# One unit of the projection in another order: side 1 takes the values first and the output gate last, and ScalarE takes the output gate last

## The reference

```python
xn = _ln(x, norm_w, norm_b)
left = xn @ left_w + left_b
right = xn @ right_w + right_b
...
left = left * jax.nn.sigmoid(xn @ lgate_w + lgate_b)
right = right * jax.nn.sigmoid(xn @ rgate_w + rgate_b)
out_gate = jax.nn.sigmoid(xn @ ogate_w + ogate_b)
out = jnp.einsum('bkjd,bkid->bijd', left, right)
out = _ln(out, onorm_w, onorm_b)
out = out @ out_w + out_b
return out * out_gate
```

## Time and profile before

| what | value |
|---|---|
| median of 3 runs | 2826.93 us (2826.92 to 2828.26) |
| the profiled execution: its own time, its span | 2826.94 us, 2825.1 us |
| busy, share of the span | PE 86%, weight load 71%, VectorE 78%, ScalarE 49%, GpSimd 36% |
| the projection's units | from about 224 us to 1010 us of the span |

### The profile page before, as it was taken

How to read it: one execution, slowest core, us unless ns; L and a number is a source line. 1 busy time by engine, 2 the same in 40 slices (tenths; PEclk the granted TensorE clock), 3 DMA queues, 4 the chain that set the end, 5 groups by cost and what they waited for, 6 DMA issues and landing times. The chain is left out here.

```text
span 2825.1 us, 42511 instructions
## 1 busy us (share of the span) xinstructions
PE 2443.7 (86%) x14742; PEld 1994.7 (71%) x14742; DVE 2209.7 (78%) x3468; ACT 1380.1 (49%) x1812; POOL 1021.5 (36%) x1043
## 2 busy tenths in 40 slices
PE   0007999999999979999999996799999989979982
PEld 0006889998989868888888885566666666778872
DVE  6998999999999758888888888777676767438852
ACT  0106999999999956766766775122122222110000
POOL 0019888888898720000000000344444444300000
PEclk9999999999999989999999998899999999869997
DMA  9944999999999777777777777999999999539999
GB/s 383 388 186 178 348 354 350 348 349 344 351 345 348 284 291 272 281 288 273 282 287 277 279 284 299 335 404 416 394 417 393 415 391 393 131 116 407 421 420 410
DMA packets 244976, 927.49 MB, mean 328 GB/s; under 512 B 18009, under 2 KB 21593, under 8 KB 244442
## 3 DMA queue, kind: packets, MB, share of 16 engines
q1 hardware_dynamic: 205912, 796.12, 74.3%
q10 hardware_dynamic: 38898, 129.21, 11.4%
HBM read 527.85 MB, written 394.92 MB: 327 GB/s over the span
## 5 line engine op out<-in xcount | busy, mean ns | idle before, releaser
L1231 POOL TENSOR_TENSOR fi_square_sum<-fi_square_sum,fi_square 128x1024 f32<-128x1024 f32 x128 | 302.8, 2366 | 359.2 <-ACT fi_square L1197 359.2
L712 DVE SCALAR_TENSOR_TENSOR pj_lr<-pj_v_ps,keep_b_val,pj_sig 128x1024 f32<-128x1024 f32 x256 | 328.4, 1283 | 91.0 <-PE pj_v_ps L565 59.5
L1197 ACT ACTIVATE fi_square<-fi_x 128x1024 f32<-128x1024 f32 x128 | 135.5, 1059 | 515.8 <-DVE fi_x L1259 513.3
L505 POOL TENSOR_TENSOR front_ring<-front_ring,front_gn_shift 128x512 f32<-128x512 f32 x256 | 329.4, 1288 | 1.0 <-DVE front_ring L678 1.0
L1152 PE MATMUL fi_y_ps<-fi_scaled,keep_w_bd 128*128 128x512 f32 x512 | 273.0, 615 | 28.0 <-DVE fi_scaled L1242 27.2
L904 PE MATMUL ct_acc_ps<-ct_l_hi,ct_r_hi 128*128 128x512 f32 x1024 | 281.0, 395 | 17.1 <-ACT ct_r_hi L927 17.1
L648 ACT ACTIVATE pj_sig<-pj_g_ps,keep_b_gate 128x1024 f32<-128x1024 f32 x256 | 285.7, 1116 | 5.7 <-PE pj_g_ps L565 2.0
L908 PE MATMUL ct_acc_ps<-ct_l_lo,ct_r_hi 128*128 128x512 f32 x1024 | 280.7, 395 | 0.0
L912 PE MATMUL ct_acc_ps<-ct_l_hi,ct_r_lo 128*128 128x512 f32 x1024 | 280.1, 394 | 0.0
L1242 DVE TENSOR_TENSOR fi_scaled<-fi_m,fi_s_ps 128x512 f32<-128x512 f32 x256 | 173.7, 679 | 134.8 <-DMA fi_m<-mixed_d 124.7
L1223 POOL MEMSET fi_square_sum<- 128x1024 f32 x1 | 1.0, 951 | 747.0 <-POOLq L780 747.0
(11 more groups left out here) (183 smaller groups left out, 6288.6 us busy)
## 6 DMA issues: line engine op xcount, KB each, us to landing
lr_d<-pj_lr SPq DMA_DIRECT2D x128, 1024.0 KB, 6.1
gate_d<-pj_gout SPq DMA_DIRECT2D x128, 512.0 KB, 6.8
ct_l<-lr_d SPq DMA_DIRECT2D x64, 1024.0 KB, 7.0
ct_r<-lr_d SPq DMA_DIRECT2D x64, 1024.0 KB, 9.0
mixed_d<-ct_o SPq DMA_DIRECT2D x64, 1024.0 KB, 5.0
fi_g<-gate_d SPq DMA_DIRECT2D x128, 512.0 KB, 15.1
fi_x<-in_x SPq DMA_DIRECT2D x32, 2048.0 KB, 17.3
fi_m<-mixed_d SPq DMA_DIRECT2D x128, 512.0 KB, 17.6
```

The lines of the kernel that those rows point to most:

```text
L505: pool.tensor_tensor(tile(m), tile(m), keep.gn_shift[:, :].unsqueeze(1).to_broadcast([P, WS // 2, C]), ALU.add).then_inc(shifted, 1)
L712: dve.scalar_tensor_tensor(out=out[:, :, RG * (m % 2):RG * (m % 2) + RG], in0=v_ps[:, :].rearrange("p (q i) -> p q i", i=RG), scalar=keep. ...
L1231: pool.tensor_tensor(square_sum[:, :, :], square_sum[:, :, :], square[:, :, :], ALU.add).then_inc(sum_done, 1)
```

## The change

It edits the order of instructions in one unit of `project`. On TensorE, behind T0, side 1 takes its value products first and those of the output gate last. V1.0 now stands in front of S0, and carries the wait for `gated`; O1.0 keeps its wait for `half_o`, five products further on. On ScalarE the operations behind the sigmoid go from `copy_rest`, `gate`, `copy_turned` to `copy_turned`, `copy_rest`, `gate`. The semaphore `vals_in` now counts both sides, so the numbers in its waits double. No operation is added or removed.

```diff
             def values(n, m, e, i):
-                if e == 0 and i == 0:
+                if e == 1 and i == 0:
                     at_least(pe, gated, n)
                 last = one(v_ps[:, L * e:L * e + L], keep.w_val, m, e, i, i == 0, i == 2)
-                if e == 1 and i == 2:
+                if i == 2:
                     last.then_inc(vals_in, 1)
...
                 if here:
-                    out_gate(n, m, 1, 0)
+                    values(n, m, 1, 0)
                 if rest:
                     subtract_high(n + 2, m + 2, 0)
                 if here:
+                    values(n, m, 1, 1)
+                    values(n, m, 0, 0)
+                    values(n, m, 1, 2)
+                    values(n, m, 0, 1)
+                    out_gate(n, m, 1, 0)
+                    values(n, m, 0, 2)
                     out_gate(n, m, 1, 1)
-                    values(n, m, 0, 0)
                     out_gate(n, m, 1, 2)
-                    values(n, m, 0, 1)
-                    values(n, m, 1, 0)
-                    values(n, m, 0, 2)
-                    values(n, m, 1, 1)
-                    values(n, m, 1, 2)
...
-                at_least(act, vals_in, n - 3)
+                at_least(act, vals_in, 2 * (n - 3))
...
             def slot(n, m, j):
                 if inside(n):
                     sigmoid(n, m)
+                if inside(n + 3):
+                    copy_turned(n + 3, m + 3)
                 if inside(n + 2):
                     copy_rest(n + 2, m + 2)
                 if inside(n):
                     gate(n, m, j)
-                if inside(n + 3):
-                    copy_turned(n + 3, m + 3)
...
-                dve.wait_ge(vals_in, n + 1)
+                dve.wait_ge(vals_in, 2 * n + 2)
```

## The result

The changed kernel takes 2923.53 us (median of 4 runs, 2922.33 to 2925.1), the kernel before 2827.6 in the same comparison; the ratio is 1.0336 (1.0324 to 1.0349). The forecast was 2942, 115 us more than before; it came to 96 us more. The direction, the place and the mechanism are as predicted, the size is 19 us too large. Against the range (2923 to 2960) it is a matter of the base: the median is 0.5 us inside, and 96 us on the 2826.9 from which the forecast started would be 2922.8, just outside.

What follows compares the result with a forecast made beforehand. The prediction saw the projection bound by a 3.024 us loop through ScalarE, side 1 of TensorE nearly equal. The new loop, 2.25 + 0.43 + 0.69 + 0.11 = 3.48, over 250 units gives 114, plus 1: 2826.9 + 115 = 2942 us, range 2923 to 2960.

Steps and rivals of the forecast that it cites:

- (d): O1.2 in the slot's last place, with one o_ps buffer: the loop through the gate takes 3.48 us a unit, 0.46 more.
- the gate is hidden after all: Rival: the wait for o_ps stays off the loop and side 1 sets the period; 0 to -10 us, chance 0.04.
- (a): TensorE's pattern of sides behind T0: each place keeps its start, an early V1.0 gains nothing; cost nothing.
- first link: From O0.0's weight load to O1.2 in the last place: 2.29 less 0.04, so 2.25 us.
- the last place comes earlier than 2.2: Sign that the forecast is wrong: O1.2 less than 2.2 us after O0.0's weight load, where 2.25 was expected.
- the weight load runs past S0's wait: Rival on TensorE: V1.1's weights load while S0 waits, period 3.31, +73 us, 2900 us; chance 0.05.
- shortest period: Bound of the loop through the gate: V1.0 early and signal links 0.03 shorter give 3.45 us a unit, +108 us.
- main case: The late O1.2 closes the projection's loop through the gate: 2931 to 2956 us, chance 0.85.
- (b): The wait for gated, moved to V1.0 in TensorE's queue: cost 0, cover about 0.3 us.
- (c): copy_turned put in front on ScalarE: pushes copy_rest by at most 0.5 us, cost 0.
- The clock: Rival in the projection: TensorE's idling lowers its clock, about +500 us more, 3440 us; chance 0.02.
- VectorE's idle time: Expected profile sign: idle before value rises from 0.34 to about 0.8 us a unit.

Runs made afterwards that it cites:

- e4: Changed kernel with the output gate taken over half of its columns from unit 8 on: 2871.9 us, ratio 1.0154 to the kernel before.
- e7: Changed kernel with two o_ps banks used in turn and VectorE's scale operand read from SBUF: 2898.99 us, ratio 1.025 to the kernel before.
- e9: Changed kernel with side 1 taking V1.0, V1.1, O1.0, O1.1, O1.2, V1.2: 2876.6 us, ratio 1.0178 to the kernel before.
- e1: Changed kernel with ScalarE kept in the old order, so TensorE's new order alone: 2924.35 us, ratio 1.0339 to the kernel before.
- e3: Changed kernel with the wait for half_o put in front of V1.0 as well: 2969.26 us, ratio 1.0496 to the kernel before.
- e8: Kernel before with two o_ps banks used in turn and VectorE's scale operand read from SBUF: 2897.4 us, ratio 1.0248 to the kernel before.
- e10: Changed kernel with side 1 taking V1.0, O1.0, O1.1, O1.2, V1.1, V1.2 and ScalarE in the old order: 2852.69 us, ratio 1.0091 to the kernel before.
- e2: Kernel before with ScalarE's new order alone, TensorE as before: 2846.01 us, ratio 1.0063 to the kernel before.
- e6: Kernel before with VectorE's scale operand read from SBUF instead of its PSUM copy, one o_ps bank: 2899.09 us, ratio 1.0247 to the kernel before.

## What the prediction had right, and what it mis-sized

**The mechanism held.** Step (d): O1.2 in the slot's last place makes O1.2, gate, g_done, O0.0 the loop. The gate's link (e4, 0.204 of 0.22), the bank (e7's undisturbed slots, 2.97 with two banks), the place (e9) and the half of the change that carries it (e1) each say so. Its links came out at 0.42, 0.69 and 0.12 for 0.43, 0.69 and 0.11. That 1.23 doesn't fit in 0.73 was the right test for the rival "the gate is hidden after all".

**The step that failed is (a), as it stands in the first link: 2.25, measured 2.18.** The prediction gave "the last place comes earlier than 2.2" as a sign of being wrong, and this sign came. Step (a) said that each place keeps its start and that "a V1.0 that is up to 0.2 early gains nothing". Taken apart: weight load of O0.0 to S1 0.58 for 0.61, S1 to S0 0.56 for 0.55, S0 to the third place 0.34 for 0.40, the three places to O1.2 0.70 for 0.69. The large piece is 0.34 for 0.40. I had read O1.1's start, 0.17 after S0's (605.31, 605.48), as the price of loading its weights behind S0's wait. In fact it stood 0.35 behind O1.0, which had waited for half_o and whose weights were loaded only as it started:

```profile
605.13 0.18 PEld L565 LDWEIGHTS pj_o_ps<-pj_high,front_w_og_high 64*128 64x128 f32 x1
```

In the changed kernel V1.0 starts at 599.98, 0.22 ahead of S0 instead of O1.0's 0.18, and its weights were loaded ahead (599.87). V1.1 is issued 0.01 after S0, and now it is V1.1 whose weights are loaded on the spot and V1.2 that follows 0.33 later. So the third place hangs on the first one and not on S0: it starts 0.58 behind it in the kernel before (605.13, 605.71), 0.56 in the changed one (599.98, 600.54), 0.54 in e3 (600.95, 601.49) and 0.57 in e8 (601.97, 602.54), while behind S0 it stands 0.40, 0.34, 0.51 and 0.36. From O0.0's weight load to the first place it was 1.02 before and is 0.92 now, 1.11 in e3, where the wait is back. That the first place comes earlier by the wait for half_o is shown by e3 in direction; the 0.03 of it that lies at T1 and S1 is read from the rows and was not tested. The other two pieces came out 0.01 longer each. So the first link is 0.07 shorter than in the sum, and the period, 3.402 for 3.48, is 0.08 shorter, which is the 19 us.

**The range** had 3.45 as its shortest period. That bound named V1.0's early start, but gave it no size; the 0.35 from O1.0 to O1.1 (605.13, 605.48) was the row for it. Another 0.06 a unit, 15 us, would have put the lower edge well under the measured time. That the time came so near the edge at all is owed to the room left below the main case, which the prediction gives no reason for.

**The rival "the weight load runs past S0's wait"** did not happen: V1.1's weights are loaded at 600.20, with S0's, not ahead. The pull-ahead across row groups that the Trainium skill describes ("TensorE: Matmul & The Clock Gate", Part 3, The mechanism) is not contradicted. The trace shows a load ahead of a product of the other half (V1.2's weights at 600.31, V0.0, ahead of it in the queue, at 600.54), but in the slots read none ahead of a wait that stood in the queue between (605.32, 600.20). The time went that rival's way, by another means.

**The other steps.** (b) gated cost nothing in this order, and e10 shows how near it was: with V1.0 early and V1.1 and V1.2 at the slot's end it closes the loop at 3.11. (c) ScalarE's order cost nothing here (e1 against the change), since its gate waits for O1.2 anyway; by itself it costs 17 us (e2), which the prediction did not look at. The clock did not fall: granted 1.00. VectorE's idle time rose to 0.63 a unit rather than 0.8: the base, 0.34, had the idle last units in it (0.27 from 260 to 960 us), and the period grew by 0.38 rather than 0.46. Side 1 of TensorE was said to close at 3.02 by itself; e8's undisturbed slots have 2.98.

## What to carry to other kernels

Where two engines hand a single buffer to and fro, count from the last write of it to the next first write: signal, reader, signal (here 1.23 us). The work that stands between those two in the writer's order must be at least that long; what is missing is paid in every unit, even if each engine shows idle time. Here 0.73 us stood between them by the old starts, so 0.50 was missing; the slot got shorter by 0.11 (2.29 to 2.18), and the change cost 0.38 a unit. A buffer with one copy therefore wants its writes close together: e10 put the values' first product early and left the last one last, and lost 0.09 a unit to the other buffer.

When a wait is taken from a place in a queue, ask what streamed late because of it: the product behind it was limited by that, not by the next wait in the row. And a test that frees a resource needs its own control: here freeing the bank cost 70 us by itself. Give the freed resource to the old order as well: without e8, the 2.95 of e7 would have passed for a gain of the new order.

## What was not expected of the hardware

With its second operand in SBUF instead of PSUM, VectorE's scale rose from 676 to 904 ns, and two operations on 64 columns from 195 to 883 and 864 ns, while GpSimd works on SBUF nearly without a break (e6). GpSimd's own two operations on 128x512 slowed as well, from 1290 to 1467 and from 1044 to 1145 ns. The Trainium skill has a rule for the first ("SBUF — State Buffer", Who interferes with whom): a VectorE instruction with two SBUF inputs contends with a GpSimd instruction that reads SBUF. The trace agrees in direction. e6's expectation had this only as its rival. What slowed the two short operations is not shown.

Idle times of TensorE's weight loads of 0.58 us in a unit of 3.4 left the granted clock at 1.00 through the changed kernel's stage. In e6, the 4 us from 478 on, in which TensorE was busy 2.29, were followed by 4 us at a granted 0.61; behind the 4 us from 610 on, with the same 2.29, it stayed at 1.00. What tells the two apart is not shown.

Where its input is there, ScalarE starts its next operation 0.10 to 0.12 us before the record of the last one ends (e2: 1.02 after a sigmoid of 1.12, 0.47 after a copy of 0.59). Records of operations that stand back to back can't be added up; their starts can.
